# Attention over 8 x 8 windows on one core: squares summed ahead of the residual's addition, the loop's turn moved by three steps, the last two images stored by step

## The chip, the cores and the metric

The kernel runs on one NeuronCore of one Trainium2 chip. The metric is the time of one execution on the device in microseconds (us). Five engines work side by side and meet at semaphores: TensorE (PE; its weight loads are a row of their own, PEld), VectorE (DVE), ScalarE (ACT), GpSimd (POOL) and the sync engine (SP), which here issues nearly all DMA transfers.

## The reference

The input x is 128 images of 224 channels by 32 x 32 pixels. Each image is normalized in 16 groups, and an attention block is applied and added to x. Cut to what matters:

```python
def _gn(v, G=16, eps=1e-5):
    g = v.reshape(B_, H_, W_, G, C_ // G)
    m = jnp.mean(g, axis=(1, 2, 4), keepdims=True)
    s = jnp.var(g, axis=(1, 2, 4), keepdims=True)
    return ((g - m) / jnp.sqrt(s + eps)).reshape(v.shape)

xh = x.transpose(0, 2, 3, 1)
q, k, v = xh @ Wq, xh @ Wk, xh @ Wv          # 224 -> 224, 8 heads of 28
# windows of 8 x 8; the 16 windows are the 16 tokens of an attention,
# one attention for each of the 64 places in a window and each head
sim = jnp.einsum('bmhid,bmhjd->bmhij', q2 * scale, k2) + pos_emb
attn = jax.nn.softmax(sim, axis=-1)
o = jnp.einsum('bmhij,bmhjd->bmhid', attn, v2)
o = o @ Wo + bo
x = x + conv(_gn(x))
```

## The kernel before

The images are handled in quarters: 512 steps of 256 tokens, four per image, and each engine walks through the same steps in an order that is written out by hand. Step t works on many stages at once: the scores and the softmax of step t, the projections to q, k and v of step t + 4 (`PROJ_LEAD`), the weighing of the values of step t - 2, the output projection of step t - 3 (`OUT_LAG`), and the addition of the result to x of step t - 4 (`FINAL_LAG`). The statistics of an image are taken 14 to 11 steps ahead: sums (L665), squares on ScalarE (L488), sums of the squares on VectorE (L672), the join of the two channel halves on GpSimd (L743, tile `both`), and the totals over partitions on TensorE (L435, tile `ps_tot`). I count the steps of an image from first (t divisible by 4) to fourth.

The order of VectorE in a step (L688 to L728) is: olo (the low half of the attention's output, L696), scores times scale plus bias (L701), the row maximum (L708), the transpose of the probabilities of the step before (L714), the residual's addition `add_out` (L684), group sums, group squares, and the sum and reciprocal of exp (L726, L728). GpSimd subtracts the maximum (L775), makes `xlo` (L786), joins (L743) and multiplies by the reciprocal (L796). ScalarE, after its exp (L552), normalizes two groups, copies k (L559), normalizes two more, adds the bias in two of four steps (L496), and makes `ohi` (L567). TensorE takes, in each step, q, v and k (L345), the scores (L376), the weighing (L388), in the first step of an image the totals (L435), and `ps_out` (L345). In the first step of an image ps_tot waits for `joined`, and ps_out waits in each step for `final`, the addition of the step before.

The steps are unrolled 48 at a time (12 images, `PERIOD`) in a loop of 10 rounds. Ahead of it stand steps -15 to 11, behind it 492 to 516, written out. The loop's head is at step 12 (`LOOP_AT`), where each engine jumps back by itself, without a barrier.

The sync engine issues in step t the loads of x, four copies of the probabilities of step t - 1 (L313), in two of four steps four copies of k (L321), and the stores: a whole channel half of an image (L271, 448 KB), at steps 4b + 7 and 4b + 8 for image b. The last image alone is stored by step, two transfers of 112 KB each (`store_rows`, L280).

Of the kernel before, what the change touches and what calls it, by code (L numbers as in the profile page):

```python
# [13 lines left out]
B, C, HH, WW = 128, 224, 32, 32  # L14
WS = 8
NW = HH // WS
TOK = HH * WW
CH, CP = 2, C // 2
# [8 lines left out]
T2 = 2  # L27
STEPS = B * TOK // (T2 * TILE)
# [12 lines left out]
XBUFS = 6  # L41
# [6 lines left out]
LOAD_LEAD, SUM_LEAD, RSQ_LEAD, TOT_LEAD, STAT_LEAD = 15, 14, 13, 12, 11  # L48
NORM_LEAD, SPLIT_LEAD, PROJ_LEAD = 9, 5, 4
PV_LAG, OUT_LAG, FINAL_LAG, STORE_LAG = 2, 3, 4, 7  # L50
# [1 line left out]
IMAGES = ROUND_BUFS * XBUFS  # L52
PERIOD = 4 * IMAGES
FIRST = -LOAD_LEAD
LOOP_AT = 12
ROUNDS = (STEPS - LOAD_LEAD - LOOP_AT) // PERIOD
LOOP_END = LOOP_AT + ROUNDS * PERIOD
LAST = STEPS + STORE_LAG - 3
# [2 lines left out]
def build(nc, x, wq, wk, wv, wo, bo, pos, scale, out):  # L61
    ctx = ExitStack()
    with ctx:
# [165 lines left out]
        def image_at(t, lead):  # L229
            b, r = divmod(t + lead, 4)  # L230
            return b if r == 0 and 0 <= b < B else None
# [20 lines left out]
        @block.sync  # L252
        def _(sp):
            n_w = 0

            def load_x(b, ch, i):
                if b is None:
                    return
                c = slice(ch * CP, ch * CP + CP)
                wait(sp, y_stored[ch][b % XBUFS], 16 * (b // XBUFS), i, 16 * ROUND_BUFS)  # L260
                sp.dma_start(x_sb[:, b % XBUFS, ch],
                             x[b + i * IMAGES, c].rearrange("p y z -> p (y z)") if isinstance(i, int)
                             else x[bass.ds(b + i * IMAGES, 1), c].rearrange("o p y z -> p (o y z)")
                             ).then_inc(x_loaded[ch][b % XBUFS], 16)

            def store_y(b, ch, i):
                if b is None:
                    return
                c = slice(ch * CP, ch * CP + CP)
                per_step(sp, final, 4 * b + 3, i)  # L270
                sp.dma_start(out[b + i * IMAGES, c].rearrange("p y z -> p (y z)") if isinstance(i, int)  # L271
                             else out[bass.ds(b + i * IMAGES, 1), c].rearrange("o p y z -> p (o y z)"),
                             x_sb[:, b % XBUFS, ch]).then_inc(y_stored[ch][b % XBUFS], 16)

            def store_rows(g, ch):

                per_step(sp, final, g, 0)
                c, r0 = slice(ch * CP, ch * CP + CP), (g % 4) * T2
                sp.dma_start(out[g // 4, c].rearrange("p (nh r) z -> p nh (r z)", nh=NW)[:, :, r0 * WW:(r0 + T2) * WW],  # L280
                             x_sb[:, (B - 1) % XBUFS, ch].rearrange("p (nh y) -> p nh y", nh=NW)[:, :, r0 * WW:(r0 + T2) * WW]
                             ).then_inc(rows_stored, 16)

            def load_weights(dst, src):
                sp.dma_start(dst, src).then_inc(weights_loaded, 16)

            load_x(0, 0, 0)
            load_x(0, 1, 0)
            for kind, w in ((0, wq), (1, wk)):
                for ch in range(CH):  # L290
                    load_weights(wqk_f[:, ch, kind * 256:kind * 256 + 256].rearrange("p (h d) -> p h d", d=DP)[:, :, 0:D],
                                 w[ch * CP:(ch + 1) * CP, :].rearrange("p (h d) -> p h d", d=D))
                    n_w += 1
            for ch in range(CH):
                load_weights(wv_f[:, ch, :], wv[ch * CP:(ch + 1) * CP, :])
                n_w += 1
            sp.wait_ge(zeroed, N_ZEROED)
            for hg in range(HG):
                for h in range(HPG):
                    row = (hg * HPG + h) * D  # L300
                    load_weights(wo_f[h * DP:h * DP + D, hg, :], wo[row:row + D, :])
                    n_w += 1
            assert n_w == N_WEIGHTS

            def step(t, i):
                if t > FIRST + 1:
                    load_x(image_at(t, LOAD_LEAD), 0, i)
                    load_x(image_at(t, LOAD_LEAD - 1), 1, i)
                g = t - 1
                if is_step(g):  # L310
                    per_step(sp, turned, g, i)
                    for pr in range(PAIRS):
                        sp.dma_start(p_bd[pr * 32:pr * 32 + 32, g % 2, pr, :],  # L313
                                     pt_f[pr * 32:pr * 32 + 32, g % 2, :]).then_inc(p_placed[g % 2], 16)
                u = t + PROJ_LEAD
                if is_step(u) and u % 2 == 1:
                    h = u // 2
                    per_step(sp, k_kept, u, i)
                    for hd in range(HPG):
                        p = slice(hd * DP, hd * DP + DP)  # L320
                        sp.dma_start(k_bd[p, h % 2, :, hd % 2, :], k_cut[p, h % 2]).then_inc(k_placed[h % 2], 16)  # L321
                if t - FINAL_LAG >= STEPS - 4:
                    if is_step(t - FINAL_LAG):
                        for ch in range(CH):
                            store_rows(t - FINAL_LAG, ch)
                if image_at(t, -STORE_LAG) != B - 1:
                    store_y(image_at(t, -STORE_LAG), 0, i)
                if image_at(t, -STORE_LAG - 1) != B - 1:
                    store_y(image_at(t, -STORE_LAG - 1), 1, i)
            rounds(sp, step)  # L330
            for ch in range(CH):
                for s in range(XBUFS):
                    sp.wait_ge(y_stored[ch][s], 16 * ((B - 1 - s + XBUFS - 1) // XBUFS))
            sp.wait_ge(rows_stored, 16 * CH * 4)

        @block.tensor
        def _(pe):
# [234 lines left out]
        def _(dve):  # L572
# [102 lines left out]
            def add_out(g, i):  # L675
                if not is_step(g):
                    return
                b = g // 4
                per_step(dve, projected, g, i)
                if g % 4 == 0:  # L680
                    per_image(dve, bias_added, b, i, CH)
                r0 = (g % 4) * T2
                xr = x_sb[:, b % XBUFS].rearrange("p ch (nh y) -> p (ch nh) y", nh=NW)[:, :, r0 * WW:(r0 + T2) * WW]
                nc.vector.scalar_tensor_tensor(  # L684
                    xr, ps_out[0:CP, :].rearrange("p (q y) -> p q y", q=CH * NW),
                    out_scale[0:CP, :], xr, ALU.mult, ALU.add).then_inc(final, 1)

            def step(t, i):  # L688
# [21 lines left out]
                if is_step(t - 1):  # L710
# [2 lines left out]
                    per_step(dve, pv_done, t - 3, i)  # L713
                    nc.vector.transpose(pt_f[:, (t - 1) % 2], sc[:, (t - 1) % 2]).then_inc(turned, 1)  # L714
                stat_op(stat_b, 3, i)
                add_out(t - FINAL_LAG, i)
                stat_op(stat_b, 4, i)
                stat_op(stat_b, 5, i)
                group_sums(image_at(t, SUM_LEAD), 0, i)
                group_sums(image_at(t, SUM_LEAD - 1), 1, i)  # L720
                group_squares(image_at(t, RSQ_LEAD), 0, i)
                group_squares(image_at(t, RSQ_LEAD - 1), 1, i)
                stat_op(stat_b, 6, i)
                if is_step(t):
                    per_step(dve, exped, t, i)
# [102 lines left out]
```

## Time and profile before

| | before |
|---|---|
| median of 3 runs | 3660.76 us (3659.74 to 3661.59) |
| profiled execution, own time | 3659.29 us |
| its span, first to last instruction | 3657.5 us |
| busy: PE, DVE, ACT, POOL | 3606.4, 3030.6, 2932.8, 2052.5 us |
| mean granted clock of TensorE | 1.000 of full speed |
| DMA | 141 GB/s, HBM 64 GB/s |

The span leaves out 1.8 us of the execution's own time. A step is about 7 us, an image about 28.1. TensorE is marked busy nearly everywhere because its matmuls overlap in the profile, so small waits between them don't show as idle time: the starts of equal groups, one image apart, tell more. In a timeline row the bracket names the idle time ahead of the row and the semaphore that came last.

### The profile page before, as it was taken

How to read it: one execution, taken by the hardware profiler on the slowest of the kernel's cores; microseconds unless marked ns; L12 is line 12 of the kernel's file. 1: busy time of each engine (PE TensorE's matmuls, PEld its weight loads, DVE VectorE, ACT ScalarE, POOL GpSimd, SP SyncE). 2: the span in 40 equal slices, each digit the busy share in tenths (PEclk: the TensorE clock that was granted, in tenths of full speed). 3: DMA queues.
4: the chain of work that ended last, by engine and by line, in shares of the span. 5: the costliest groups of instructions: out<-in, count | busy, mean ns of one | idle time of the engine just before them, and what ended most of it. 6: DMA issues, size and time to landing. Idle time of an engine off the chain costs nothing.

```text
span 3657.5 us, 168559 instructions
## 1 busy us (share of the span) xinstructions
PE 3606.4 (99%) x68610; PEld 2623.1 (72%) x68610; DVE 3030.6 (83%) x5027; ACT 2932.8 (80%) x5377; POOL 2052.5 (56%) x3335
## 2 busy tenths in 40 slices
PE   6999999999999999999999999999999999999998
PEld 4777777777777777777777777777777777777776
DVE  6888888888888888888888888888888888888886
ACT  7888888888888888888888888888888888888884
POOL 5555555555555555555555555555555555555553
PEclk9999999999999999999999999999999999999999
DMA  4555555555555555555555555555555555555544
GB/s 105 144 137 144 145 146 135 149 142 146 135 146 145 145 136 145 146 146 135 145 145 145 135 146 145 145 136 147 144 145 136 146 145 145 135 146 145 145 126 120
DMA packets 255773, 515.36 MB, mean 141 GB/s; under 512 B 66352, under 2 KB 66800, under 8 KB 254992
## 3 DMA queue, kind: packets, MB, share of 16 engines
q1 hardware_dynamic: 253456, 504.35, 52.7%
q8 instruction: 555, 9.09, 1.1%
q14 instruction: 226, 1.85, 0.2%
q10 hardware_dynamic: 1536, 0.07, 0.0%
HBM read 118.31 MB, written 117.44 MB: 64 GB/s over the span
## 4 chain that ended last, share of the span: by engine, by line
PE 38%; issue 25%; POOL 18%; DVE 11%; ACT 7%; POOLq 1%; SPq 0%; DVEq 0%; DMA 0%; ACTq 0%
PE ps_out L345 8%; PE ps_q L345 7%; PE ps_k L345 7%; PE ps_v L345 6%; PE ps_o L388 5%; POOL sc L775 5%; ACT xn L510 5%; POOL xlo L786 4%; PE ps_s L376 4%; POOL newton L757 4%; DVE part L672 3%; POOL sc L796 3%; DVE sc L701 2%; DVE pt_f L714 2%; DVE x_sb L684 2%
## 5 line engine op out<-in xcount | busy, mean ns | idle before, releaser
L775 POOL TENSOR_TENSOR sc<-sc,mx 128x512 f32<-128x512 f32 x512 | 537.3, 1049 | 864.2 <-DVE mx L708 864.2
L510 ACT ACTIVATE xn<-x_sb,norm_add,norm_mul 112x128 f32<-112x128 f32 x2048 | 1012.2, 598 | 0.0
L696 DVE TENSOR_TENSOR olo<-ps_o,ohi 128x512 f16<-128x512 f32 x512 | 353.8, 691 | 542.5 <-ACT ohi L567 533.4
L796 POOL TENSOR_TENSOR sc<-sc,rs 128x512 f32<-128x512 f32 x512 | 537.3, 1049 | 425.0 <-DVE rs L728 424.9
L345 PE MATMUL ps_out<-ohi,wo_s 128*112 128x256 f16 x4096 | 721.3, 278 | 2.6 <-DVE x_sb L684 2.4
L552 ACT ACTIVATE sc<-sc 128x512 f32<-128x512 f32 x512 | 323.3, 632 | 461.3 <-POOL sc L775 460.9
L345 PE MATMUL ps_q<-xhi,wqk 112*128 112x512 f16 x2048 | 611.2, 380 | 6.6 <-issue 3.7
L345 PE MATMUL ps_k<-xhi,wqk 112*128 112x512 f16 x2048 | 609.2, 379 | 0.8 <-ACT k_cut L559 0.8
L345 PE MATMUL ps_v<-wv_s,xhi 112*128 112x224 f16 x4096 | 560.4, 259 | 0.0
L388 PE MATMUL ps_o<-p_bd,v_sb 128*32 128x128 f32 x16384 | 553.6, 276 | 4.8 <-DMA p_bd<-pt_f 3.8
L786 POOL TENSOR_TENSOR xlo<-xn,xhi 112x1024 f16<-112x1024 f32 x256 | 547.3, 2138 | 16.5 <-ACT xhi L533 14.8
L376 PEld LDWEIGHTS ps_s<-k_bd,q_sb 64*32 64x32 f32 x32768 | 357.1, 105 | 219.3 <-issue 217.2
L345 PEld LDWEIGHTS ps_out<-ohi,wo_s 128*112 128x112 f16 x4096 | 448.1, 130 | 85.0 <-issue 78.4
L345 PEld LDWEIGHTS ps_v<-wv_s,xhi 112*128 112x128 f16 x4096 | 396.0, 98 | 121.5 <-issue 0.6
L388 PEld LDWEIGHTS ps_o<-p_bd,v_sb 128*32 128x32 f32 x16384 | 416.6, 109 | 53.1 <-DMA p_bd<-pt_f 5.1
L376 PE MATMUL ps_s<-k_bd,q_sb 64*32 64x64 f32 x32768 | 439.9, 224 | 2.8 <-DVE sc L701 2.8
L539 ACT ACTIVATE q_sb<-ps_q 128x512 f32<-128x512 f32 x512 | 300.5, 587 | 127.1 <-PE ps_q L345 125.1
L345 PE MATMUL ps_out<-olo,wo_s 128*112 128x256 f16 x2048 | 391.4, 273 | 0.0
L701 DVE SCALAR_TENSOR_TENSOR sc<-ps_s,s_scale,pos_sb 128x512 f32<-128x512 f32 x512 | 379.8, 742 | 0.0
L684 DVE SCALAR_TENSOR_TENSOR x_sb<-ps_out,out_scale,x_sb 112x512 f32<-112x512 f32 x512 | 366.4, 716 | 3.5 <-PE ps_out L345 1.7
L345 PE MATMUL ps_v<-wv_s,xlo 112*128 112x224 f16 x2048 | 363.8, 259 | 0.0
L708 DVE TENSOR_REDUCE mx<-sc 128x16 f32<-128x512 f32 x512 | 351.3, 686 | 13.2
(78 smaller groups left out, 5733.2 us busy)
## 6 DMA issues: line engine op xcount, KB each, us to landing
k_bd<-k_cut SPq DMA_DIRECT2D x1024, 128.0 KB, 2.5
p_bd<-pt_f SPq DMA_DIRECT2D x2048, 64.0 KB, 2.4
x_sb<-in_x SPq DMA_DIRECT2D x256, 448.0 KB, 4.3
out_y<-x_sb SPq DMA_DIRECT2D x254, 448.0 KB, 3.6
out_y<-x_sb SPq DMA_DIRECT2D x8, 112.0 KB, 2.5
k_cut<-in_L_conv_Wq SPq DMA_DIRECT2D x2, 98.0 KB
k_cut<-in_L_conv_Wk SPq DMA_DIRECT2D x2, 98.0 KB
k_cut<-in_L_conv_Wv SPq DMA_DIRECT2D x2, 98.0 KB
```

Source lines behind the costliest of these rows:

```text
L345: last = nc.tensor.matmul(dst, w_parts(a, ch), x_parts(c, ch), start=(n == 0), stop=(n == 3 * chunks - 1))
L376: last = nc.tensor.matmul(ps_s[pr * 32:pr * 32 + 32, half, col:col + 64].rearrange("p (h j) -> p h j", j=32), q_sb[rows, h % QBUFS, hg, to ...
L388: last = nc.tensor.matmul(ps_o[h * 32:h * 32 + 32, col:col + 128].rearrange("p (r j) -> p r j", j=32), v_sb[:, g % VBUFS, t2, hg * HPG + h ...
L510: nc.scalar.activation(xn[:, b % 2, :, c4, :, :, nw].rearrange("p r c q -> p q r c"), x_sb[:, b % XBUFS].rearrange("p ch (nh r w) -> p (ch ...
L552: nc.scalar.activation(sc[:, t % 2], sc[:, t % 2], ACT.Exp).then_inc(exped, 1)
L684: nc.vector.scalar_tensor_tensor(xr, ps_out[0:CP, :].rearrange("p (q y) -> p q y", q=CH * NW), out_scale[0:CP, :], xr, ALU.mult, ALU.add). ...
L696: nc.vector.tensor_tensor(olo[:, g % 2], in_x_order(ps_o[:, :]), ohi[:, g % 2], ALU.subtract).then_inc(o_lo, 1)
L701: nc.vector.scalar_tensor_tensor(sc[:, t % 2].rearrange("p (a c) -> p a c", a=2), ps_s[:, :, 0:256], s_scale[:, :], pos_sb[:].rearrange("p ...
L708: nc.vector.reduce_max(mx[:, t % 2], rows, axis=AX.X).then_inc(maxed, 1)
L775: nc.gpsimd.tensor_tensor(rows, rows, mx[:, t % 2].unsqueeze(2).broadcast_to(by_row), ALU.subtract).then_inc(shifted, 1)
L786: nc.gpsimd.tensor_tensor(by_channel_half(xlo[:, h % 2]), half_of_xn(h), by_channel_half(xhi[:, h % 2]), ALU.subtract).then_inc(x_lo, 1)
L796: nc.gpsimd.tensor_tensor(rows, rows, rs[:, t % 2].unsqueeze(2).broadcast_to(by_row), ALU.mult).then_inc(probs, 1)
```

## The change

Three edits. On VectorE the sum of the squares of the second channel half (only in the first step of an image) stands ahead of the residual's addition. The loop's head moves from step 12 to step 15, so each engine jumps back between the third and the fourth step of an image, and three steps more are written out ahead of the loop and three fewer behind it. The last two images, not only the last, are stored by step.

```diff
-LOOP_AT = 12
+LOOP_AT = 15
+
+WHOLE = B - 2
 ROUNDS = (STEPS - LOAD_LEAD - LOOP_AT) // PERIOD
...
-                             x_sb[:, (B - 1) % XBUFS, ch].rearrange("p (nh y) -> p nh y", nh=NW)[:, :, r0 * WW:(r0 + T2) * WW]
+                             x_sb[:, (g // 4) % XBUFS, ch].rearrange("p (nh y) -> p nh y", nh=NW)[:, :, r0 * WW:(r0 + T2) * WW]
...
-                if t - FINAL_LAG >= STEPS - 4:
+                if t - FINAL_LAG >= 4 * WHOLE:
                     if is_step(t - FINAL_LAG):
                         for ch in range(CH):
                             store_rows(t - FINAL_LAG, ch)
-                if image_at(t, -STORE_LAG) != B - 1:
-                    store_y(image_at(t, -STORE_LAG), 0, i)
-                if image_at(t, -STORE_LAG - 1) != B - 1:
-                    store_y(image_at(t, -STORE_LAG - 1), 1, i)
+                for ch in range(CH):
+                    whole = image_at(t, -STORE_LAG - ch)
+                    if whole is not None and whole < WHOLE:
+                        store_y(whole, ch, i)
...
                 stat_op(stat_b, 3, i)
+
+                group_squares(image_at(t, RSQ_LEAD - 1), 1, i)
                 add_out(t - FINAL_LAG, i)
                 stat_op(stat_b, 4, i)
                 stat_op(stat_b, 5, i)
                 group_sums(image_at(t, SUM_LEAD), 0, i)
                 group_sums(image_at(t, SUM_LEAD - 1), 1, i)
                 group_squares(image_at(t, RSQ_LEAD), 0, i)
-                group_squares(image_at(t, RSQ_LEAD - 1), 1, i)
```

VectorE's program where the loop begins, before: the end of a fourth step, the loop's head (L206), and the first step of an image (L198 and ISA are registers for the waits).

```order
L672 TENSOR_REDUCE part<-sq 112x16
L726 TENSOR_REDUCE sm<-sc 128x16
L728 RECIPROCAL rs<-sm 128x16
L206 UNCONDITIONAL_BRANCH
L206 BRANCH_PREFETCH_HINT
L206 ISA
L696 TENSOR_TENSOR olo<-ps_o,ohi 128x512
L198 REGISTER_ALU x2
L701 SCALAR_TENSOR_TENSOR sc<-ps_s,s_scale,pos_sb 128x512
```

The same place after the change (lines are two higher): the end of a third step, the loop's head (L208), and the beginning of the fourth.

```order
L729 TENSOR_REDUCE sm<-sc 128x16
L731 RECIPROCAL rs<-sm 128x16
L208 UNCONDITIONAL_BRANCH
L208 BRANCH_PREFETCH_HINT
L208 ISA
L698 TENSOR_TENSOR olo<-ps_o,ohi 128x512
L200 REGISTER_ALU x2
L703 SCALAR_TENSOR_TENSOR sc<-ps_s,s_scale,pos_sb 128x512
L710 TENSOR_REDUCE mx<-sc 128x16
```

The head, and with it the jump, now has the third step's reciprocal ahead of it and the fourth step's olo behind it. The other place is VectorE in the first step of an image, from the row maximum to the reciprocal, before:

```order
L708 TENSOR_REDUCE mx<-sc 128x16
L198 REGISTER_ALU
L714 STREAM_TRANSPOSE pt_f<-sc 128x512
L198 REGISTER_ALU
L198 ISA
L684 SCALAR_TENSOR_TENSOR x_sb<-ps_out,out_scale,x_sb 112x8x64
L198 REGISTER_ALU
L672 TENSOR_REDUCE part<-sq 112x16
L726 TENSOR_REDUCE sm<-sc 128x16
L728 RECIPROCAL rs<-sm 128x16
```

And after, with the squares (L674) ahead of the addition (L686):

```order
L703 SCALAR_TENSOR_TENSOR sc<-ps_s,s_scale,pos_sb 128x512
L710 TENSOR_REDUCE mx<-sc 128x16
L716 STREAM_TRANSPOSE pt_f<-sc 128x512
L200 REGISTER_ALU
L674 TENSOR_REDUCE part<-sq 112x16
L200 REGISTER_ALU
L686 SCALAR_TENSOR_TENSOR x_sb<-ps_out,out_scale,x_sb 112x8x64
L729 TENSOR_REDUCE sm<-sc 128x16
L731 RECIPROCAL rs<-sm 128x16
```

In this step the two have changed places, and the sum over exp (L729) stands behind both as before.

The sync engine's last instructions, before (L313 copies of probabilities, L271 a whole store, L280 a store by step):

```order
L271 DMA out_y<-x_sb 112x1024
L313 DMA p_bd<-pt_f 32x512 x4
L271 DMA out_y<-x_sb 112x1024
L313 DMA p_bd<-pt_f 32x512 x12
L271 DMA out_y<-x_sb 112x1024
L313 DMA p_bd<-pt_f 32x512 x4
L280 DMA out_y<-x_sb 448x1x64 x2
L271 DMA out_y<-x_sb 112x1024
L280 DMA out_y<-x_sb 448x1x64 x6
```

And after:

```order
L273 DMA out_y<-x_sb 112x1024
L315 DMA p_bd<-pt_f 32x512 x4
L282 DMA out_y<-x_sb 448x1x64 x2
L273 DMA out_y<-x_sb 112x1024
L315 DMA p_bd<-pt_f 32x512 x4
L282 DMA out_y<-x_sb 448x1x64 x2
L315 DMA p_bd<-pt_f 32x512 x4
L282 DMA out_y<-x_sb 448x1x64 x2
L315 DMA p_bd<-pt_f 32x512 x4
L282 DMA out_y<-x_sb 448x1x64 x2
L315 DMA p_bd<-pt_f 32x512 x4
L282 DMA out_y<-x_sb 448x1x64 x8
```

The two whole stores of image 126 (L271 in the last but two and in the last places) are gone, and four pairs of stores by step stand between the copies; the one whole store left there is image 125's.

## Rows read from the trace of the kernel before

**Rows 1.** The page: busy time by engine, and the engines' shares of the chain.

```profile
PE 3606.4 (99%) x68610; PEld 2623.1 (72%) x68610; DVE 3030.6 (83%) x5027; ACT 2932.8 (80%) x5377; POOL 2052.5 (56%) x3335
...
PE 38%; issue 25%; POOL 18%; DVE 11%; ACT 7%; POOLq 1%; SPq 0%; DVEq 0%; DMA 0%; ACTq 0%
```

**Rows 2.** Table of waits: who waited for whom, us in total, times, longest us.

```profile
ACT sc L552 <- POOL sc L775: 460.9, 500, 3.6
...
DVE olo L696 <- ACT ohi L567: 533.4, 394, 3.0
...
PE ps_tot L435 <- POOL both L743: 23.9, 9, 11.3
...
ACT ohi L567 <- PE ps_o L388: 9.9, 6, 3.5
...
DVE x_sb L684 <- issue: 1.6, 1, 1.6
```

**Rows 3.** Timeline of TensorE, an image's first step: start us, us, instruction.

```profile
2018.08 0.60 PE L345 MATMUL ps_q<-xhi,wqk 112*128 112x512 f16 x2
...
2023.71 0.26 PE L435 MATMUL ps_tot<-both,ones 112*32 112x32 f32 x8
...
2025.26 0.60 PE L345 MATMUL ps_q<-xhi,wqk 112*128 112x512 f16 x2
```

**Rows 4.** Timeline of TensorE, a first step in which nothing was waited for.

```profile
1032.94 0.60 PE L345 MATMUL ps_q<-xhi,wqk 112*128 112x512 f16 x2
...
1038.46 0.24 PE L435 MATMUL ps_tot<-both,ones 112*32 112x32 f32 x8
...
1038.63 0.42 PE L345 MATMUL ps_out<-ohi,wo_s 128*112 128x256 f16 x2
...
1039.99 0.60 PE L345 MATMUL ps_q<-xhi,wqk 112*128 112x512 f16 x2
...
1046.98 0.60 PE L345 MATMUL ps_q<-xhi,wqk 112*128 112x512 f16 x2
```

**Rows 5.** Timelines of ScalarE, VectorE and GpSimd, fourth step and following first step.

```profile
2015.49 0.63 ACT L552 ACTIVATE sc<-sc 128x512 f32<-128x512 f32 x1 [0.47 <-POOL sc L775]
...
2018.14 0.63 ACT L567 ACTIVATE ohi<-ps_o 128x512 f16<-128x512 f32 x1
...
2018.80 0.69 DVE L696 TENSOR_TENSOR olo<-ps_o,ohi 128x512 f16<-128x512 f32 x1
...
2021.41 0.71 DVE L684 SCALAR_TENSOR_TENSOR x_sb<-ps_out,out_scale,x_sb 112x512 f32<-112x512 f32 x1
...
2022.05 1.21 DVE L672 TENSOR_REDUCE part<-sq 112x16 f32<-112x1024 f32 x1
...
2020.95 1.05 POOL L775 TENSOR_TENSOR sc<-sc,mx 128x512 f32<-128x512 f32 x1 [1.11 <-DVE mx L708]
...
2023.33 0.25 POOL L743 TENSOR_TENSOR both<-part 112x32 f32<-112x32 f32 x1 [1.33 <-DVE part L672]
```

**Rows 6.** Timeline of GpSimd, the subtraction; a turn lies behind 1817.18.

```profile
1767.51 1.05 POOL L775 TENSOR_TENSOR sc<-sc,mx 128x512 f32<-128x512 f32 x1 [1.10 <-DVE mx L708]
...
1795.62 1.05 POOL L775 TENSOR_TENSOR sc<-sc,mx 128x512 f32<-128x512 f32 x1 [1.09 <-DVE mx L708]
...
1817.18 1.05 POOL L775 TENSOR_TENSOR sc<-sc,mx 128x512 f32<-128x512 f32 x1 [1.54 <-DVE mx L708]
...
1824.18 1.05 POOL L775 TENSOR_TENSOR sc<-sc,mx 128x512 f32<-128x512 f32 x1 [1.57 <-DVE mx L708]
```

**Rows 7.** Timeline of VectorE, olo of a fourth step and at the turn.

```profile
1815.03 0.69 DVE L696 TENSOR_TENSOR olo<-ps_o,ohi 128x512 f16<-128x512 f32 x1 [1.21 <-ACT ohi L567]
...
1822.03 0.69 DVE L696 TENSOR_TENSOR olo<-ps_o,ohi 128x512 f16<-128x512 f32 x1 [0.54 <-ACT ohi L567]
```

**Rows 8.** Timeline of the sync engine's issues near the end.

```profile
3642.54 0.57 SPq L271 DMA_DIRECT2D out_y<-x_sb  x1
...
3644.13 2.41 SPq L313 DMA_DIRECT2D p_bd<-pt_f  x4
```

More of the change, by code:

```diff
@@ L332, in _ @@
                 for s in range(XBUFS):
-                    sp.wait_ge(y_stored[ch][s], 16 * ((B - 1 - s + XBUFS - 1) // XBUFS))
-            sp.wait_ge(rows_stored, 16 * CH * 4)
+                    sp.wait_ge(y_stored[ch][s], 16 * ((WHOLE - s + XBUFS - 1) // XBUFS))
+            sp.wait_ge(rows_stored, 16 * CH * 4 * (B - WHOLE))
         @block.tensor
```

## Prediction

> **What bounds the kernel now.** I read the page first, then the table of waits, then the timeline of one image, and last the place where the loop jumps back. The page shows TensorE busy for 99% of the span, which invites the conclusion that TensorE is the bound and that every wait taken from it is won. The chain of the same page says otherwise: TensorE has 38% of it, GpSimd 18%, VectorE 11%, ScalarE 7%, and 25% is "issue" [rows 1]. A pure TensorE bound would show nearly nothing else.
>
> In the table of waits the reader is to see a circle [rows 2]: ScalarE's exp waits for GpSimd's subtraction in 500 of 512 steps, VectorE's olo waits for ScalarE's ohi in 394, and ohi waits for TensorE in only 6. So step after step runs ohi, olo, scores plus bias, row maximum, subtraction, exp, and behind the exp, without idle time, the normalization and k_cut on ScalarE, and ohi again. Nothing in this circle waits for TensorE. The stretch of one step shows it whole: exp at 2015.49, ohi at 2018.14, olo at 2018.80, the next subtraction at 2020.95 [rows 5]. I call it the softmax circle. It takes 28.11 us per image (1795.62 less 1767.51, [rows 6]).
>
> TensorE's own pace stands in an image in which it found both ready: the step with the totals takes 7.05 us (1039.99 less 1032.94), an ordinary one 6.99 (1046.98 less 1039.99) [rows 4], so 7.05 + 3 x 6.99 = 28.02 us per image. It is 0.09 us per image quicker than the circle. That difference comes out as a wait ahead of ps_tot: "both" ends at 2023.33 + 0.25 = 2023.58, ps_tot starts at 2023.71 (0.13 us of signalling), and the step takes 2025.26 - 2018.08 = 7.18 us [rows 3, 5]. So TensorE waits about 0.1 us once per image because it is ahead of the circle; were the wait taken away, it would only be further ahead.
>
> **The squares ahead of the residual's addition.** No instruction is added. In the first step of an image the addition (start 2021.41) and the reduction of the squares (start 2022.05) change places [rows 5]. From start to start the addition takes 0.64 us, so "both" is ready 0.64 us earlier, at 2022.94. TensorE reaches ps_tot at about ps_q + 5.52 (1038.46 less 1032.94, [rows 4]), here 2023.60, so the wait for "both" goes. What is late next is the addition itself: it moves back by the reduction's 1.21 less the 0.07 by which neighbours on VectorE overlap here (2021.41 + 0.71 against 2022.05), so by 1.14, and ends at 2021.41 + 1.14 + 0.71 = 2023.26; with the 0.13 of signalling TensorE could have it at 2023.39. It wants it for ps_out at ps_q + 5.69 (1038.63 less 1032.94), here 2023.77. That is 0.38 us of room, and TensorE eats 0.09 of it per image, so after four or five images it waits again as long as before, now for x_sb. GpSimd's join and the sum over exp stand behind both operations as before, and the squares were made on ScalarE a step earlier. Value of the swap in the steady loop: 0. Bounds: from below 0.09 x 119 images = 10.7 us gained, if TensorE did set the pace; on the other side 0.
>
> **The turn of the round.** The loop jumps back nine times and is entered once. Now it does so ahead of the first step of an image. There ohi ends when VectorE has just finished the step before, and olo follows with no idle time (no bracket behind 2018.80, [rows 5]). At a turn the row of the same place shows 0.54 us of idle time ahead of olo [rows 7]. The profile names ohi for it because that is the semaphore in the instruction, but ohi was as early as ever; it is the jump. The circle then has nothing to hide it: from the subtraction at 1795.62 to that at 1824.18 are 28.56 us, 0.45 more than 28.11 [rows 6]. After the change the jump falls between the third and the fourth step. There olo waits 1.21 us for ohi anyway [rows 7], and 0.54 fits in with 0.67 to spare. Gain: 10 x 0.45 = 4.5 us, taking the entry as a tenth turn. Bounds: 0 if the circle pays the jump at the new place too, 10 x 0.54 = 5.4 if it had paid all of it. GpSimd's jump falls into the 1.54 us that it waits ahead of the fourth step's subtraction (at 1817.18, [rows 6]). ScalarE's is not to be seen in any row; there the new place is narrower, 0.47 us of idle time ahead of the fourth step's exp [rows 5]. Were its jump as dear as VectorE's and not run ahead of, 10 x (0.54 - 0.47) = 0.7 us would come back; I take 0, the upper end is kept. TensorE's own jumps are covered by its being ahead. On the sync engine the jump is past the transfers of a step and ahead of the next; it waits for VectorE's transpose in most steps, so nothing is behind it.
>
> On instruction fetch the trace has two prices: the jump's 0.54 [rows 7], and a stretch of 1.6 us behind the loop in which VectorE waited before the addition for nothing that the profile shows [rows 2]. I read the second as code that was not there yet. The Trainium skill (Runtime: NRT & Kernel Launch, section Instruction fetch mechanics) says that an engine holds only two blocks of code, fetched in sequence, and that a taken branch whose target is outside of them has to wait for a transfer. By that rule moving the head of the loop is no free act: it is the third rival below. That the jumps so far cost a third of 1.6 us speaks for a target fetched in time, and the new code is still closed by the same hinted jump, so I leave the sum as it is.
>
> **The last two images by step.** Image 126 was stored by two transfers of 448 KB, now by eight of 112 KB, two per step, each pair behind the step's four copies of probabilities. An issue takes about 0.57 us on the sync engine, and a whole-channel store at 3642.54 is followed by the next copies at 3644.13 [rows 8]: between 3643.11 and 3644.13 there is 1.02 us, and two issues instead of one need 0.6 more. It fits. Only where the store of image 125 stands in the same step may a copy of probabilities start some 0.4 us late (my estimate: 3 x 0.6 of issues into a step that has about 1.4 free), and TensorE has that set one step later; I take 0, bounds 0.6 to either side (one issue more or less). The last four stores and their landing, which end the program, are the same as before.
>
> **Sum.** Own time of the profiled execution 3659.29 us (span 3657.5). Less 4.5 for the turns, 0 for the swap, 0 for the stores: 3654.8. The median of the runs is 1.47 above the profiled execution, so 3656.3. The case's own range: gain of the turns 0 to 5.4, ScalarE's 0.7, stores 0.6, and one code wait of 1.6 behind the loop that may come or go, combined to 3653 to 3659 (two of them seldom fall together).
>
> **Rivals.**
> A. TensorE is the bound after all, so the swap pays in every image: for it speak 99% busy and the wait ahead of ps_tot; against it the circle without a wait for TensorE. Time: 3656.3 - 10.7 = 3645.6.
> B. The jump is paid at the new place as well, because ScalarE's or VectorE's jump delays the circle there (the work of the fourth step is the heaviest on VectorE, with both reductions). Then nothing is gained: 3660.8. For it: ScalarE's thin 0.47. Against: 1.21 on VectorE.
> C. Slower: at the new head the code of an engine in the circle is not there, and each of the nine turns and the entry waits as the place behind the loop does, 1.6 us [rows 2], in a stretch that hides nothing, such as ScalarE's from exp to ohi. 10 x 1.6 = 16, less the 4.5: 3660.8 + 11.5 = 3672. It decides from 0.45 us unhidden per turn on; above that the kernel is slower than before. Nothing in the trace of before shows such a turn.
> D. The swap doesn't unblock TensorE at all since the addition takes the place of "both" at once: same time as the forecast, since the swap counts for 0 there.
>
> **How the numbers follow.** Forecast (with D) 0.70, A 0.10, B 0.13, C 0.07. A measurement of this kernel can tell about 0.2%, 7.3 us. The forecast's 4.5 is within it: faster than 3653.4 are A and a small part of the forecast's spread, 0.13; slower than 3668.1 is most of C, 0.06; the same is the rest, 0.81. Range 3650 to 3661: the forecast's own range, B, and a part of the way to A.
>
> **What would show it.** In the changed profile: the waits of ps_tot for both, 9 so far with 23.9 us [rows 2] of which the start has the most, gone except there; the small one of every image was never in that table, and its successor ahead of ps_out need not be either. The subtraction still 28.11 us apart per image, and 28.11 to 28.15, not 28.56, across a turn. Ahead of olo in the fourth step, 1.2 us of idle time at a turn as elsewhere. The first step of an image still 7.13 to 7.18 us on TensorE. The forecast is wrong if the images are 28.02 apart (A), if a turn still costs 0.4 or more (B), or if an idle time of over 1 us follows each jump (C).

## The result: slower by 0.24%, and the profile after

| | before | after |
|---|---|---|
| median of the runs, side by side | 3662.18 us (10 runs, 3659.74 to 3663.49) | 3671.90 us (10 runs, 3663.83 to 3673.92) |
| profiled execution's own time | 3659.29 us | 3673.92 us |
| span | 3657.5 us | 3672.1 us |

The ratio is 1.0024, 95% interval 1.0016 to 1.0032. The forecast was 3656.3 us. It was wrong in sign: by the medians the change costs 9.7 us. The profiled execution is the slowest of its ten, so the profile shows more loss (14.6 us) than the median.

The page of the changed kernel, busy time by engine and the chain by engine (answers to [rows 1]):

```profile
PE 3607.3 (98%) x68610; PEld 2631.2 (72%) x68610; DVE 3032.1 (83%) x5027; ACT 2926.8 (80%) x5377; POOL 2049.0 (56%) x3335
...
PE 97%; issue 1%; ACT 1%; SPq 1%; DMA 0%; DVE 0%; POOL 0%; ACTq 0%; DVEq 0%; POOLq 0%
```

No engine works more than before. The chain has moved from a mixture to TensorE, but that must not be read as "TensorE is now the bound": TensorE and the circle differ by 0.1 us per image, and a chain followed backward stays on the one of two such neighbours where it happens to arrive. The table of waits says more (answers to [rows 2]; us in total, times, longest us):

```profile
DVE olo L698 <- ACT ohi L569: 528.8, 392, 4.3
...
PE ps_tot L437 <- POOL both L746: 22.1, 2, 11.5
...
ACT ohi L569 <- PE ps_o L390: 16.5, 8, 6.7
...
PE ps_q L347 <- issue: 11.9, 11, 1.5
...
PE ps_o L390 <- DMA p_bd<-pt_f: 7.4, 3, 4.7
...
PE ps_s L378 <- issue: 2.9, 1, 2.9
```

The circle is as it was (olo waits for ohi 392 times, 394 before), and ps_tot waits for "both" twice, at the start, where it waited nine times. The three last rows are new or have grown. "Issue" means that the engine waits for nothing that the profile shows. TensorE does so eleven times ahead of ps_q and once ahead of the scores, and it waits up to 4.7 us for the copies of probabilities. The table of before has no such row for ps_s, and two small ones for the others:

```profile
PE ps_o L388 <- DMA p_bd<-pt_f: 3.8, 4, 1.6
PE ps_q L345 <- issue: 3.7, 5, 1.0
```

**An image in the loop** (TensorE's first step, answers to [rows 3]; then "both", the squares' reduction and the residual's addition of the same step, to [rows 5]):

```profile
2023.01 0.60 PE L347 MATMUL ps_q<-xhi,wqk 112*128 112x512 f16 x2
...
2028.52 0.24 PE L437 MATMUL ps_tot<-both,ones 112*32 112x32 f32 x8
...
2030.05 0.60 PE L347 MATMUL ps_q<-xhi,wqk 112*128 112x512 f16 x2
```

```profile
2026.38 1.18 DVE L674 TENSOR_REDUCE part<-sq 112x16 f32<-112x1024 f32 x1
...
2027.48 0.74 DVE L686 SCALAR_TENSOR_TENSOR x_sb<-ps_out,out_scale,x_sb 112x512 f32<-112x512 f32 x1
...
2027.64 0.25 POOL L746 TENSOR_TENSOR both<-part 112x32 f32<-112x32 f32 x1 [0.67 <-DVE part L674]
```

"Both" ends at 2027.89, 0.63 us ahead of ps_tot. The step takes 7.04 us (7.18 in [rows 3]); the addition ends at 2028.22, 5.21 behind ps_q, and is wanted at 5.69. TensorE no longer waits here.

**A turn.** GpSimd's subtraction around the first turn, which lies behind 490.06 (to [rows 6]), and VectorE's olo at it (to [rows 7]):

```profile
482.55 1.05 POOL L778 TENSOR_TENSOR sc<-sc,mx 128x512 f32<-128x512 f32 x1 [3.21 <-DVE mx L710]
...
490.06 1.05 POOL L778 TENSOR_TENSOR sc<-sc,mx 128x512 f32<-128x512 f32 x1 [0.85 <-DVE mx L710]
...
511.60 1.05 POOL L778 TENSOR_TENSOR sc<-sc,mx 128x512 f32<-128x512 f32 x1 [3.91 <-DVE mx L710]
...
539.78 1.05 POOL L778 TENSOR_TENSOR sc<-sc,mx 128x512 f32<-128x512 f32 x1 [3.21 <-DVE mx L710]
```

```profile
494.43 0.69 DVE L698 TENSOR_TENSOR olo<-ps_o,ohi 128x512 f16<-128x512 f32 x1 [1.20 <-ACT ohi L569]
```

The image with the turn takes 511.60 - 482.55 = 29.05 us, the next one 28.18; before it was 28.56 against 28.11. Yet olo waits 1.20 us at the turn, as in any fourth step: VectorE's jump is hidden, exactly as planned. What is late stands on TensorE and, behind it, on ScalarE:

```profile
485.98 0.60 PE L347 MATMUL ps_q<-xhi,wqk 112*128 112x512 f16 x2
...
494.50 0.60 PE L347 MATMUL ps_q<-xhi,wqk 112*128 112x512 f16 x2 [1.37 <-issue]
```

```profile
496.08 0.60 ACT L541 ACTIVATE q_sb<-ps_q 128x512 f32<-128x512 f32 x1 [0.74 <-PE ps_q L347]
...
503.11 0.60 ACT L541 ACTIVATE q_sb<-ps_q 128x512 f32<-128x512 f32 x1 [1.90 <-PE ps_q L347]
```

The step takes 494.50 - 485.98 = 8.52 us instead of 6.99, 1.53 more. Over the nine turns this excess is 1.53, 1.53, 1.12, 1.62, 0.75, 1.71, 1.66, 0.45 and 1.17 us (before: 0.45 at most, 0 at four of them), and the taken branch in TensorE's queue lasts 1.6 to 2.8 us (before: 1.0 to 1.6). TensorE's small lead is used up, ScalarE gets q late, and the circle loses some 0.9 us of it (29.05 against the 28.13 of the median image).

The trace also has the transfers of code. They stand in DMA queues of their own, called "instruction" in the profile; q8 carries packets of 16 KB, and at a turn the branch follows them. The jump back begins at 491.58 and ends at 494.24. Between 487.00 and 491.50 the queue has no packet; the one that counts begins at 491.75, 0.17 us behind the branch's start. Its row in the stretch from 491.5 to 492 (packets, MB, share of 16 engines):

```profile
q8 instruction: 1, 0.02, 11.7%
```

That is 0.117 x 16 x 0.5 = 0.94 us, so the packet ends at 492.69, and the branch 1.55 us later. At all nine turns here the branch ends 1.4 to 1.6 us behind the end of such a packet, and at the nine of before 1.4. The packets are no longer than they were (1.11 us on average, 1.09 before), but they begin 0.20 us ahead of the branch on average, and before 1.28.

**Behind the loop**, one step after its end, TensorE's stream stops in the midst of the scores; then two stretches of time (start and end, length, busy us and count of TensorE's matmuls and weight loads, VectorE, ScalarE and GpSimd, and last the granted clock, the DMA engines' mean busy share and GB/s):

```profile
3541.02 0.30 PE L378 MATMUL ps_s<-k_bd,q_sb 64*32 64x64 f32 x5
3544.27 1.13 PE L378 MATMUL ps_s<-k_bd,q_sb 64*32 64x64 f32 x59 [2.95 <-issue]
```

```profile
3543.00:3551.00 8.00, 6.73 (x109) 5.36 (x109) 5.11 (x9) 2.34 (x6) 2.90 (x3) 0.57 0.60 152
3551.00:3558.00 7.00, 7.00 (x141) 5.29 (x140) 2.91 (x6) 5.85 (x11) 1.46 (x3) 1.00 0.38 105
```

The granted clock falls to the lower level (1.2 GHz) at 3543.20, within the stop of 2.95 us, and stays there for 6.8 us: a mean of 0.57 over 8 us is 6.9 us at half. That step takes 12.61 us; the step behind the exit took 7.07 before.

**At the end** the sync engine's issues (to [rows 8]), and the row of TensorE that hangs on them:

```profile
3651.73 5.40 SPq L315 DMA_DIRECT2D p_bd<-pt_f  x4
...
3657.18 1.44 SPq L282 DMA_DIRECT2D out_y<-x_sb  x2
```

```profile
3658.62 1.39 PE L390 MATMUL ps_o<-p_bd,v_sb 128*32 128x128 f32 x32 [4.66 <-DMA p_bd<-pt_f]
```

Four copies take 5.40 us there, not 2.41: 2.8 us lie between the issues of the third and the fourth, in which the engine waits for no semaphore.

**The sum of the two profiled executions**, 14.6 us apart: the rounds, 338.22 against 337.82 us (mean of the eight from the first turn to the ninth), and nine turns: 3.6. The step behind the loop: 5.5. The end, from the addition of step 507 to that of step 511 (16.1 against 13.1): 3.0. And 2.4 near the start, where the granted clock of this execution is at half for 6.8 us; that last one comes and goes between kernels with the same code there, so I don't count it to the change. Together 14.5.

### The profile page after: what moved, and what is told of

The parts are those of the page before. It is cut to its first block, busy times and chain, and to the rows that moved or that the text cites. A ratio compares the mean times of both kernels' runs of the same rounds, so it can differ in the third digit from the quotient of the medians.

```text
span 3672.1 us, 168555 instructions
## 1 busy us (share of the span) xinstructions
PE 3607.3 (98%) x68610; PEld 2631.2 (72%) x68610; DVE 3032.1 (83%) x5027; ACT 2926.8 (80%) x5377; POOL 2049.0 (56%) x3335
## 3 DMA queue, kind: packets, MB, share of 16 engines
q14 instruction: 254, 2.08, 0.2%
## 4 chain that ended last, share of the span: by engine, by line
PE 97%; issue 1%; ACT 1%; SPq 1%; DMA 0%; DVE 0%; POOL 0%; ACTq 0%; DVEq 0%; POOLq 0%
PE ps_out L347 20%; PE ps_q L347 18%; PE ps_k L347 18%; PE ps_v L347 16%; PE ps_o L390 14%; PE ps_s L378 11%; ACT xn L512 0%; SPq L287 0%; PE ps_tot L437 0%; SPq L315 0%; DMA x_sb<-in_x 0%; DMA p_bd<-pt_f 0%; POOL xlo L789 0%; ACT xhi L535 0%; DVE sc L703 0%
## 5 line engine op out<-in xcount | busy, mean ns | idle before, releaser
L686 DVE SCALAR_TENSOR_TENSOR x_sb<-ps_out,out_scale,x_sb 112x512 f32<-112x512 f32 x512 | 370.5, 724 | 4.8 <-PE ps_out L347 3.1
```

What stands on the lines that cost most here:

```text
L686: nc.vector.scalar_tensor_tensor(xr, ps_out[0:CP, :].rearrange("p (q y) -> p q y", q=CH * NW), out_scale[0:CP, :], xr, ALU.mult, ALU.add). ...
```

## Experiments

All times are medians, each beside the kernel before in the same job. "Idle at the turns" is the excess over 6.99 us of the TensorE step with the turn.

**1. The squares alone.** Turn at 12 and stores as before.

```
                 stat_op(stat_b, 3, i)
+                group_squares(image_at(t, RSQ_LEAD - 1), 1, i)
                 add_out(t - FINAL_LAG, i)
...
-                group_squares(image_at(t, RSQ_LEAD - 1), 1, i)
```

> Only the squares ahead of the addition; the turn and the stores as before. Circle theory (the softmax circle of ScalarE, VectorE and GpSimd sets 28.12 us per image, TensorE only waits for it): the same time within 1.5 us, the subtraction on GpSimd still 28.12 apart, the turn still 0.44 dearer. Rival (TensorE sets the pace): 10.7 us faster, images 28.02 apart.

Measured: 3657.69 us against 3659.59; ratio 0.9995, 0.9986 to 1.0004. In the trace the image takes 28.09 us (28.12 before) and the round 337.56 (337.82). This part does no harm; whether its 2 us are real the ratio doesn't tell.

**2. The turn alone.**

```
-LOOP_AT = 12
+LOOP_AT = 15
```

> Only the turn of the loop at step 15; squares and stores as before. Code theory (TensorE's code for the head of the loop is fetched behind the copies of k and the load of x of the third step, and comes 1.5 us late; at the loop's exit the next block comes late by 3 us and more): TensorE idle 1 to 1.5 us ahead of ps_q at most of the nine turns, rounds about 338.2 instead of 337.8 us, over 3 us lost at step 495, 5 to 10 us slower than before. Rival (the swap is what costs): as fast as before or 4 us faster.

Measured: 3666.53 us; ratio 1.0017, 1.0008 to 1.0026. The first turn:

```profile
494.91 0.60 PE L345 MATMUL ps_q<-xhi,wqk 112*128 112x512 f16 x2 [1.11 <-issue]
```

Eight of nine turns have 1.0 to 1.6 us idle, the branch takes up to 2.9, the round 338.55 us. The loss sits in the moved turn; the swap of squares and addition isn't needed for it. The expected stop behind the loop didn't come: the step behind the exit takes 7.05 us.

**3. The stores by step alone.**

```
+WHOLE = B - 2
...
-                if t - FINAL_LAG >= STEPS - 4:
+                if t - FINAL_LAG >= 4 * WHOLE:
...
```

> Only the last two images stored by step. Theory (the sync engine has six transfers more in the last steps, its next block of code is fetched between the copies of the probabilities of step 510, and TensorE waits for these copies): 3 to 5 us slower, all of it behind step 508, with a hole of 2 to 3 us in the sync engine's issues. Rival (the late stores cost nothing, what was seen at the end is chance): the same within 1 us.

Measured: 3661.66 us; ratio 1.0005, 0.9996 to 1.0014. The end is 1.1 us later than before (addition of step 511), and only 0.45 us of that arise behind step 507 (13.51 us from there to step 511, 13.06 before). The last three sets of four copies take 2.5 to 2.9 us, the two ahead of them 3.1 and 3.6: no 5.40. A loss of several microseconds from the stores by themselves fell. With the turn alone (experiment 2) there is none of it either. So the hole of 2.8 us appears only with the stores and the moved turn together.

**4. The whole change, with the head of the loop elsewhere in its block of TensorE's code.** TensorE's code comes in blocks: from 1000 to 1700 us of the changed kernel q8 has 108 packets of 16 KB, one per 6.5 us, with some 250 of TensorE's instructions to each. The kernel pads so that the head of the loop stands at a slot (the place of an instruction in its block) that it names.

```
-HEAD_SLOT = 104
+HEAD_SLOT = 160
```

> The changed kernel with the loop's head on TensorE at slot 160 of its block of code instead of 104, so that the loop's end lies 56 slots deeper in its last block and the head's block is asked for earlier ahead of the jump. Code theory: the idle time of 1 to 1.5 us ahead of ps_q at the turns goes, a round takes 337.4 us (12 x 28.12), and the kernel is 4 to 8 us faster than the changed one. Rival (the jump itself costs at this place, wherever the code lies): turns as in the changed kernel.

Measured: 3657.49 us; ratio 0.9994, 0.9985 to 1.0003, against 1.0024 of the change with slot 104. Both sets of code do the same work in the same order. TensorE at the turn (behind 482.06), and the circle around it:

```profile
482.06 0.60 PE L347 MATMUL ps_q<-xhi,wqk 112*128 112x512 f16 x2
...
489.05 0.60 PE L347 MATMUL ps_q<-xhi,wqk 112*128 112x512 f16 x2
...
496.11 0.60 PE L347 MATMUL ps_q<-xhi,wqk 112*128 112x512 f16 x2
```

```profile
478.69 1.05 POOL L778 TENSOR_TENSOR sc<-sc,mx 128x512 f32<-128x512 f32 x1 [3.21 <-DVE mx L710]
...
506.76 1.05 POOL L778 TENSOR_TENSOR sc<-sc,mx 128x512 f32<-128x512 f32 x1 [3.22 <-DVE mx L710]
```

6.99 us for the step of the turn, no idle time at any of the nine, the branch takes 0.36, and the image with the turn 28.07. The round is 337.08 us, 1.14 less than in the changed kernel. The row of q8 from 483.0 to 483.5, with the branch at 487.66:

```profile
q8 instruction: 1, 0.02, 20.0%
```

This packet lasts 0.200 x 16 x 0.5 = 1.6 us and begins 4.5 us ahead of the branch, as at every turn of this kernel (4.4 to 4.6). Together with the packets of the changed kernel this settles that TensorE's code was late. How a slot becomes an instant isn't shown: 56 slots are some 1.5 us of TensorE's instructions, the packet begins 4.3 us earlier. The hole behind the loop is now 2.08 us, without the clock's fall; the one at the end (2.7) is still there.

**5. The best parts together**: squares ahead, turn at 15, slot 160, stores as before.

> Squares ahead of the addition, turn at step 15, TensorE's head at slot 160; the stores as before. If the theories of the turn (code for the head late) and of the end (the sync engine's code between the copies) both hold, the parts add: no idle time on TensorE at the turns, a round 337.1 us, no hole in the sync engine's issues, and 5 to 8 us faster than before (3652 to 3655 us). Rival (the end's loss comes with the turn's place, not with the stores): as slow as with the stores, 3657 us.

Measured: 3656.76 us against 3662.56; ratio **0.9984, 0.9975 to 0.9993**. This version beats both kernels. Against experiment 4 it differs in the stores alone: the hole at the end is gone, and from the addition of step 507 to that of 511 are 13.1 us, not 16.2. The round takes 337.06 us, and VectorE's olo at the turn is at 1.20 us of idle time as in every image:

```profile
494.41 0.69 DVE L696 TENSOR_TENSOR olo<-ps_o,ohi 128x512 f16<-128x512 f32 x1 [1.20 <-ACT ohi L567]
```

**6. The same with the turn at 12.** Against experiment 5 only `LOOP_AT = 12` differs.

> Squares ahead of the addition, TensorE's head at slot 160, turn at step 12 as before. Separates TensorE's jump from VectorE's: TensorE's stalls of 0.1 to 0.9 us at the turns go. If VectorE's jump in the circle is worth 0.44 us per turn, a round stays at 12 x 28.09 + 0.44 = 337.5 us and the kernel is 3 to 5 us slower than with the turn at 15. Rival (only TensorE's code mattered): a round 337.1 us at step 12 too.

Measured: 3663.79 us; ratio 1.0004, 0.9995 to 1.0013. TensorE's turns are free here as well (under 0.1 us, branch 0.36 to 0.38), so VectorE's jump stands alone:

```profile
471.13 0.69 DVE L696 TENSOR_TENSOR olo<-ps_o,ohi 128x512 f16<-128x512 f32 x1 [0.59 <-ACT ohi L567]
```

The round takes 337.66 us against 337.06, 0.60 more. The image with the turn takes 28.56 us on average, against 28.09 in experiment 5, so 0.47 of the 0.60 is VectorE's jump; the rest is spread over the other images. The other part of the difference is behind the loop: a stop of 3.85 us (2.16 in experiment 5), within which the clock falls to half for 6.8 us:

```profile
3512.80 0.61 PE L345 MATMUL ps_q<-xhi,wqk 112*128 112x512 f16 x1 [3.85 <-issue]
```

```profile
3511.00:3519.00 8.00, 6.21 (x23) 3.23 (x23) 3.58 (x5) 2.21 (x5) 1.30 (x2) 0.57 0.43 113
```

**7. The sync engine's code shifted.** The changed kernel with 80 waits that are met already, ahead of the sync engine's steps; they take up 40 instructions (the trace has 5076 of the sync engine instead of 5036).

```
+            for _ in range(80):
+                sp.wait_ge(zeroed, N_ZEROED)
```

> The changed kernel with 80 waits (40 instructions) that are already fulfilled on the sync engine ahead of its steps, so that its blocks of code end some four steps earlier in the end part. Theory (code of the sync engine late between the copies of step 510): the hole of 2.8 us in its issues and TensorE's wait of 4.7 us for p_bd go from there, 3 to 5 us faster than the changed kernel, turns unchanged. Rival (the six more transfers themselves are too much for the queue): hole or wait stay at the same step.

Measured: 3670.64 us; ratio 1.0023, 1.0014 to 1.0032. The copies at the end take 2.46 us again, without any other change:

```profile
3646.21 2.46 SPq L318 DMA_DIRECT2D p_bd<-pt_f  x4
```

and from the addition of step 507 to that of 511 are 13.1 us as before the change. The hole hasn't vanished, it has moved with the code, to a set of copies 37 us earlier that takes 4.87 us:

```profile
3609.35 4.87 SPq L318 DMA_DIRECT2D p_bd<-pt_f  x4
```

In this kernel, and in the five others that have the hole of step 510 (the changed one and experiments 4, 8, 9 and 10), it ends 1.0 to 1.2 us behind the end of an 8 KB packet of code in queue q14. So it is a late block of the sync engine's code, not the stores. The median shows next to nothing of the 3 us, which I can't explain: the turns of this kernel vary from 0 to 1.66 us, and their spread covers it. The two profiled executions can't be compared for it either, this one being the fastest of its kernel's eleven and that of the changed kernel the slowest of ten.

**8. One load of x earlier**, ahead of the key copies that precede the turn.

```
+                if t > FIRST:
+                    load_x(image_at(t, LOAD_LEAD), 1, i)
```

> The changed kernel with the load of x's second channel half issued one step earlier in the program, ahead of the four copies of k instead of behind them, so that it is 2.8 us earlier and no longer in flight when TensorE's code for the head is asked for. Theory (that fetch stands behind the transfers of x): TensorE's idle time at the turns falls from 1.5 to below 0.7 us, a round to 337.5 us or less, 3 to 6 us faster than the changed kernel. Rival (the fetch is late for another reason, such as when it is asked for): the stalls stay at 1 to 1.5 us.

Measured: 3670.33 us; ratio 1.0019, 1.0010 to 1.0028. Idle at the turns 0.83 to 1.65 us. The theory that the code stands behind this one load fell. But the data had only changed places: in the 7 us ahead of the end of the turn's step the DMA engines' share was 0.70, as in the changed kernel:

```profile
483.60:490.60 7.00, 6.47 (x130) 4.67 (x128) 5.58 (x10) 5.59 (x11) 4.94 (x15) 1.00 0.70 173
```

**9. The data of those two steps left out.** Instructions and waits stay, the four key copies and two loads of x in the last two steps of a round move one partition each.

```
+                light = LOOP_AT + PERIOD - 2 <= t < LOOP_AT + PERIOD
-                        p = slice(hd * DP, hd * DP + DP)
+                        p = slice(hd * DP, hd * DP + (1 if light else DP))
```

> The changed kernel, but in the last two steps of a round the sync engine's four key copies and its two loads of x move one partition each instead of 32 or 128 (most of their data is left out, so some keys and some of x are not renewed). The instructions, the waits and the code are the same. Theory F (the transfer that brings TensorE's code for the head of the loop is asked for early enough, but crawls because these data move at the same time): the idle time of TensorE at the nine turns, 0.45 to 1.71 us in the changed kernel, falls to under 0.3, and the taken branch to under 1.5 us. Time 11 to 12 us under the changed kernel: 3659 to 3662. Theory T (it is late because of the place of the branch in TensorE's own code, whatever else is moved): idle time 1 to 1.6 us as before, time 3667 to 3673.

Measured: 3661.43 us against 3662.53; ratio 0.9998, 0.9989 to 1.0007. The same 7 us in before, in the changed kernel and in this one:

```profile
461.60:468.60 7.00, 7.00 (x134) 5.09 (x133) 5.73 (x10) 6.53 (x14) 5.14 (x10) 1.00 0.21 53
```

```profile
486.20:493.20 7.00, 6.93 (x132) 4.90 (x130) 6.00 (x10) 5.59 (x11) 4.48 (x14) 1.00 0.69 173
```

```profile
484.00:491.00 7.00, 7.00 (x134) 5.03 (x133) 5.98 (x12) 5.59 (x11) 4.14 (x13) 1.00 0.20 48
```

DMA share 0.21, 0.69 and 0.20; idle at the turns 0.10, 1.28 and 0.15 us on average; branch 1.2, 2.4 and 1.3 us. With the same code at the same slot the idle time is all but gone. So the code is late because of the four key copies (128 KB each) and the loads of x (448 KB each), which fall into the microseconds ahead of the turn at 15 and not of the turn at 12. The transfer doesn't crawl, as my theory had it; it begins later. The row of q8 in this kernel from 488.5 to 489, with the branch at 489.84:

```profile
q8 instruction: 1, 0.02, 12.7%
```

That is 1.02 us, not less than the 0.94 of the changed kernel, but it begins 1.2 us ahead of the branch instead of 0.2 behind its start. Over the nine turns the packets last 1.07 us on average (1.11 in the changed kernel) and begin 1.20 us ahead of the branch (0.20). What holds the packet back while the engines are busy no row shows. In experiment 4 the share is 0.64, nearly as high, and nothing waits, since the packet begins 4.5 us ahead. That is a second way out.

**10. Slot 56**, otherwise the changed kernel.

> The changed kernel with the head of the loop at slot 56 of its block of TensorE's code instead of 104, so that the branch back stands some 48 instructions earlier in its block too. Theory T (the instant at which the code is asked for, set by the place in the block, decides): the earlier place makes it worse, or the same if 104 was late already: the branch takes over 2.7 us, idle time at the turns over 1.7 us in most, round over 338.5, time 3674 to 3682. Theory F (only the data in flight decide, and those last at the turn whatever the slot): turns as in the changed kernel, 1.0 to 1.6 us, time 3668 to 3674.

Measured: 3680.47 us; ratio 1.0053, 1.0039 to 1.0067. Idle 1.63 to 2.41 us, branch 2.7 to 3.5, round 339.61. The packet begins 0.56 us behind the branch's start on average. Behind three of the turns the granted clock is at half for 3.4 us.

```profile
491.19 0.60 PE L347 MATMUL ps_q<-xhi,wqk 112*128 112x512 f16 x2 [1.49 <-issue]
```

**11. Experiment 5 with slot 216.**

> Squares ahead, turn at step 15, whole stores as before, head of the loop at slot 216 (160 in the fastest version so far). Where a later slot gives the code for the head and for the exit more time: turns without idle time as at 160, the hole behind the loop under 2.0 us (2.16 at 160), time 3654 to 3657. Where the block of the head is then left too soon (only 40 instructions behind the head until the next block is needed): idle time within 1 us behind each turn, time 3660 to 3670.

Measured: 3687.93 us; ratio 1.0067, 1.0054 to 1.0081. Idle 2.29 to 3.87 us, branch 3.3 to 5.0, round 341.52.

```profile
496.81 0.60 PE L345 MATMUL ps_q<-xhi,wqk 112*128 112x512 f16 x2 [3.71 <-issue]
```

Behind six of its nine turns the granted clock is at half for 3.4 to 6.8 us. With 56, 104, 160 and 216 the idle time at the turn is 2.0, 1.3, 0 and 2.9 us on average. Of these four 160 is best; a later one is not simply better. Both ways count, the slot and the data in flight. At 216 a packet begins 4.6 us ahead of the first turn's branch, much as in experiment 4, but the branch ends 1.6 us behind the end of a second one that begins 2.16 us behind its start. That fits my guess that the block behind the head is wanted at once, but which block a packet holds isn't recorded, and it was not separated.

## Why the prediction was wrong

**What bounds the kernel: right.** The circle stayed at 28.13 us per image (median in the loop, 28.12 before) while TensorE's first step fell to 7.05 (7.14 before), and nothing was gained from the latter. Rival A (3645.6) is out.

**The squares: the value nearly right, one step of the reasoning wrong.** The wait for "both" went and the addition fits, as worked out. But TensorE was to eat up the room in four or five images and to wait again as long as before, now for x_sb, with first steps of 7.13 to 7.18 us. In experiment 1 they take 7.05 or 7.06 us in 85 of 103 images, and the addition keeps ending 5.44 us behind ps_q, 0.12 ahead of need. Part of TensorE's waiting went over to the fourth step, which takes 7.02 us on average away from the turns (6.99 before); what it waits for there wasn't traced. Value 0 was forecast; experiment 1 has 28.09 instead of 28.12 us per image, which no step of mine gives and which the ratio can't tell from nothing.

**VectorE's jump: right.** 1.20 us of idle time ahead of olo at the turn, as foretold, and 0.47 us gained in the image with the turn where nothing else interferes (experiments 5 and 6); the forecast had 0.45 of at most 0.54. The 0.60 us per round are above that bound by something that I didn't foresee.

**The step that failed: "TensorE's own jumps are covered by its being ahead."** I gave it one sentence and no price. It needed two: how long the jump takes, and how far ahead TensorE is. Its branch already took 1.0 to 1.6 us before, with up to 0.45 us idle, so the cover was used up at some turns. The table of before said as much, had I gone down to it: ps_q waits five times for nothing that the profile shows, 3.7 us in all, once at the loop's entry (132.39) and once at a turn (1145.72). I had counted two prices of instruction fetch, both VectorE's. At the new place the branch takes 1.6 to 2.8 us, and the idle time of 1.28 us on average turns -4.5 us into +3.6 for the rounds. I had followed the sync engine's transfers past the turn for their own sake ("nothing is behind it"), but had not asked what else uses the DMA engines at that instant: TensorE's code does. On the row of a jump the Trainium skill (Runtime: NRT & Kernel Launch, section Instruction fetch mechanics) says that a taken branch to code outside the two held blocks waits for a transfer. The trace agrees only in part: with slot 104 the branch ends 1.4 to 1.6 us behind the end of a packet of code, and with slot 160 the same branch at the same place in the work waits not at all (0.36 us, experiment 4), its packet having begun 4.5 us ahead.

**Rival C had the time (3672) but not the cause; the number is luck.** It placed the missing code on an engine of the circle, 1.6 us in a stretch that hides nothing, and so 16 us in ten turns. It is TensorE, outside the circle, and the turns make only 3.6 of the 14.6 us.

**What I left out altogether: the exit and the end.** I had "one code wait of 1.6 behind the loop that may come or go". Behind the exit TensorE stopped for 2.95 us, to which the halved clock adds 2.6 (5.5 in all). That the moved exit is the cause is not shown: with the turn at 15 six kernels have a stop of 2.1 to 3.0 us there and three have none (experiments 2, 9 and 11), and the longest, 3.85, comes with the turn at 12 (experiment 6). It is late code again: in all seven kernels with a stop it ends 1.2 to 1.5 us behind the end of a packet in q8. For the sync engine I priced issues, 0 with 0.6 to either side; the issues did fit, but a late block of its code cost 3.0 in the profiled run. My range, 3650 to 3661, had taken its size from the single code wait that I had seen.

Still open: why the stop behind the loop is 0 in one kernel, 2.08 in another and 3.85 in a third, since it was never varied alone and each kernel has one profiled execution; and why experiment 7's median didn't follow its repaired end.
